# One memset more behind a block's scatters: GpSimd clears a spare tile after both of them in blocks 0 to 11

## The reference, cut to what matters

```
x = x + layernorm(attention(layernorm(x)))          # out = (q . sum k v) / (q . sum k)
x = x + layernorm(ffn(layernorm(x)))
ffn(x):
    shared = gelu(x @ Wfc_s + bfc_s) @ Wproj_s + bproj_s
    probs  = softmax(x @ Wr);  top 2, weights divided by their sum
    routed = sum over the two chosen experts e of
             weight_e * (gelu(x @ Wfc[e] + bfc[e]) @ Wproj[e] + bproj[e])
    return shared + routed
```

## Time and profile before

| | |
|---|---|
| median of three runs | 384.76 us |
| the profiled execution | 383.89 us, span 382.0 us |
| mean granted TensorE clock | 0.958 |
| PE busy | 336.9 us (88%) |
| DVE busy | 289.2 us (76%) |
| ACT busy | 256.6 us (67%) |
| POOL busy | 284.4 us (74%), 381 instructions |
| memsets of `spare` | 47, 20.6 us in all |

### The profile page before, as it was taken

The page is one execution under the profiler, slowest core; times in us unless marked ns, Lnnn a source line. Parts: engine busy times, 40 slices in busy tenths (PEclk is TensorE's granted clock), DMA queues, the critical chain, the costliest instruction groups (busy, mean ns, idle before and its releaser), DMA issues.

```text
span 382.0 us, 8164 instructions
## 1 busy us (share of the span) xinstructions
PE 336.9 (88%) x2497; PEld 292.0 (76%) x2497; DVE 289.2 (76%) x688; ACT 256.6 (67%) x692; POOL 284.4 (74%) x381
## 2 busy tenths in 40 slices
PE   7879797998999998989898995958999999989991
PEld 2538485796886868768598894948999999989971
DVE  4999999799999899999936663524554459787667
ACT  4949864887986978767246764216556666688764
POOL 8877898578788787888768888874666767866640
PEclk9969996999999999999999999886999999999997
DMA  6576767575473406143188387945788879988317
GB/s 194 166 218 168 174 180 123 115 207 133 145 194 104 140 29 199 36 135 101 33 257 259 113 226 204 243 149 159 217 263 257 251 242 367 350 246 263 125 52 205
DMA packets 53522, 69.18 MB, mean 181 GB/s; under 512 B 6365, under 2 KB 37386, under 8 KB 53482
## 3 DMA queue, kind: packets, MB, share of 16 engines
q1 hardware_dynamic: 47556, 58.58, 53.9%
q0 software_dynamic: 4544, 9.35, 7.2%
q10 hardware_dynamic: 1382, 0.79, 0.8%
HBM read 40.06 MB, written 18.15 MB: 152 GB/s over the span
## 4 chain that ended last, share of the span: by engine, by line
PE 39%; DVE 17%; ACT 11%; POOL 11%; issue 10%; another core or an unknown queue 6%; SPq 2%; DMA 2%; DVEq 0%; ACTq 0%; POOLq 0%
PE bS L1550 7%; PE bO L1550 7%; PE bO L1334 6%; DVE KV L1701 3%; ACT hs L1024 2%; DVE KV L1692 2%; POOL expert_lists L707 2%; DVE SH L2071 2%; PE bV L1523 2%; POOL Z L789 2%; PE bV L1525 2%; PE bV L1524 2%; DVE w_lo L2124 1%; POOL Z L794 1%
## 5 line engine op out<-in xcount | busy, mean ns | idle before, releaser
L830 POOL DMA_INDIRECT expert_results<-yb,yrow x78 | 77.5, 994 | 39.5 <-issue 19.2
L707 POOL DMA_INDIRECT expert_lists<-rows,pos x64 | 64.3, 1004 | 19.7 <-issue 17.7
L1701 DVE TENSOR_TENSOR_SCAN KV<-bS,KV 128x1024 f32<-128x1024 bf16 x32 | 72.8, 2277 | 0.6 <-POOL KV L733 0.3
L1334 PEld LDWEIGHTS bO<-wout_rot,Z 128*128 128x128 f32 x512 | 60.5, 192 | 8.1 <-POOL Z L789 4.5
L1334 PE MATMUL bO<-wout_rot,Z 128*128 128x128 f32 x512 | 63.0, 277 | 1.9 <-POOL Z L789 1.1
L2148 DVE COPY yrow<-xb 128x2 int32<-128x2 int32 x24 | 6.8, 284 | 47.0 <-PE bS L1550 17.0
L1153 ACT ACTIVATE hs<-bV,KV 128x256 f32<-128x256 f32 x56 | 21.9, 474 | 21.1 <-remote 10.0
L1550 PE MATMUL bO<-KV,hs 128*128 128x128 f32 x232 | 29.2, 276 | 2.9 <-ACT hs L1153 1.9
L1550 PEld LDWEIGHTS bO<-KV,hs 128*128 128x128 f32 x232 | 27.5, 192 | 3.6 <-ACT hs L1153 3.4
L1304 PE MATMUL bA<-w2s_sb,hs 128*128 128x128 f32 x224 | 28.8, 277 | 0.0
L1523 PE MATMUL bV<-x_lo,w_hi 128*128 128x256 f32 x80 | 24.4, 305 | 4.2 <-DVE x_lo L2127 3.5
(11 more groups left out here) (370 smaller groups left out, 997.4 us busy)
## 6 DMA issues: line engine op xcount, KB each, us to landing
KV<-packed_weights SPq DMA_DIRECT2D x21, 578.0 KB
Z<-packed_weights SPq DMA_DIRECT2D x18, 578.0 KB
xb<-expert_lists SPq DMA_DIRECT2D x39, 129.0 KB
vr<-vr SPq DMA_DIRECT2D x16, 224.0 KB, 2.5
shared<-expert_results SPq DMA_DIRECT2D x7, 512.0 KB
vr<-vr SPq DMA_DIRECT2D x16, 192.0 KB
vr<-vr SPq DMA_DIRECT2D x16, 160.0 KB
vr<-vr SPq DMA_DIRECT2D x16, 128.0 KB
```

The costliest lines, as they stand in the source:

```text
L707: g.indirect_dma_start(out=lists, out_offset=bass.IndirectOffsetOnAxis(ap=pos[:, m:m + 1], axis=0), in_=rows[:, m // TILES, m % TILES, :], ...
L830: g.indirect_dma_start(out=results, out_offset=bass.IndirectOffsetOnAxis(ap=yrow[n][:, c], axis=0), in_=yb[n][:, c, :], in_offset=None).th ...
L1334: ins = t.matmul(bO[:, j * D:(j + 1) * D], Z[:, d, j * P:(j + 1) * P], wout_rot[:, d], start=False, stop=True, skip_group_check=True)
L1701: v.tensor_tensor_scan(w, ps_keep, w, 0.0, ALU.mult, ALU.add).then_inc(s["kv_sum"], 1)
```

## The change

`SINGLE` is 2 x 6 = 12. In the blocks 0 to 11 `still()` follows both scatters of a block; in the blocks 12 to 26 it stands between the two as before, and from block 27 on there is none.

```
             AT_END = 4
             PAIRED = 27
+            SINGLE = 2 * NBUF
...
                         in_=yb[n][:, c, :], in_offset=None).then_inc(blk_scat[n], 16)
-                    if b < PAIRED and c == 0:
+                    if b < SINGLE or b < PAIRED and c == 0:
                         still()
```

## The result

The changed kernel takes **0.9943** of the time before (95% interval 0.9922 to 0.9963): 380.94 us against 382.91, medians of 20 runs each. By this ratio it is 2.2 us faster (1.4 to 3.0), about half the 4.0 us forecast; it leaves out executions that count as slow, one of the changed kernel's (384.26 us) among them, and the medians, which do not, are 1.97 us apart. That 380.8 was met almost to the digit is partly luck: the median of the three runs shown before lay 1.9 us above that of the 20.

What follows compares the result with a forecast made beforehand. Late TensorE signals, from GpSimd scatters directly following each other, were taken to cost blocks 3 to 11 up to 16.7 us. Net of later late blocks, 4.0 us off 383.89 gave 379.9, plus 0.87 a median of 380.8 us; range 370 to 387.

Steps and rivals of the forecast that it cites:

- the buffers bind: Block 8 needs block 2's buffer, whose second scatter ends at 243.7 plus 2.5 us landing, so it comes at 246.2.
- the debt: GpSimd's scatter work lagging VectorE at block 12, forecast at 12.5 us, to be worked off in the blocks behind.
- The way back: From block 12, single memsets again: late blocks of 7.4 us each until GpSimd has caught up at block 17.9, 289.1 us.
- The sum of 3.1 to 5.9 us: Net time earlier once GpSimd has caught up at block 17.9; everything after block 27 shifts along.
- the return: Time regained in blocks 3 to 11 by prompt signals at 3.42 us per block; block 11 14.5 us earlier.
- The choice of 4.0: Net saving in us taken for the whole kernel, nearer the lower end of 3.1 to 5.9.
- The price of up to 5.3 us: Twelve added memsets of 0.44 us each holding up VectorE's copies through the shared port, without VectorE's idle time.
- The whole return stays: Rival: signals stay prompt after block 12 too; block 11 14.5 us earlier, 370 us; chance 0.20.
- The memset does nothing: Rival: lateness comes from something coinciding, DMA traffic or GpSimd being behind; today's time plus up to 1 us, 384.8; chance 0.22.
- the gaps shrink: Rival: memsets leave 0.16 us free instead of 0.30; blocks 3 to 8 5.0 us slower, 390 us; chance 0.16.

Runs made afterwards that it cites:

- 27: Changed kernel with the memset behind both scatters in blocks 0 to 26, not only 0 to 11; ratio 1.0025 to the kernel before, 385.0 us.
- 18: Changed kernel with the memset behind both scatters in blocks 0 to 17, not only 0 to 11; ratio 0.9882 to the kernel before.
- read-back later: Changed kernel with memsets behind both scatters in blocks 0 to 26 and the read-back of results 1 to 2 blocks later; ratio 0.9899 to the kernel before.

## Why the prediction was right, and where it was off

**The cause.** The prediction put the late signals down to scatters too close together. The runs without memsets and with short ones bear that out. From block 2's addition to block 8's the kernel before takes 36.1 us. With gaps of 0.30 to 0.48 us between all block scatters it is 36.5 to 38.6, whatever stands in them; with 0.58 to 0.72 it is 24.9 to 29.7. The ratios agree: 1.0056 to 1.0131 with the short gaps, 0.9882 to 1.0033 with the long ones (without the run that adds memsets in the earlier iterations), though the intervals of the nearest two overlap. One profile alone does not size the effect: four kernels whose GpSimd program is the same up to block 11 (changed, 27, 18, read-back later) had 8.4, 3.6, 17.6 and 30.6 us of unnamed waits from 222 to 262 us. Traffic alone is not the cause: the DMA share is 0.96 in the first slow stretch now, with fewer late signals than at 0.81. The Trainium skill (DMA: Bandwidth & Descriptors, section "Issuing engines are not separate DMA queues") has all queues share the same engines; that may hold here, but by these two rows it is not what delayed the signals.

**Blocks 3 to 8.** Forecast: 3.42 us each until the buffers bind, block 8 at 246.2. Measured: 4.3 each, block 8 at 248.86 with a "remote" wait in front. I took the memset's gap as enough, from the stretch 201 to 222 us; it is at the edge, and 8.4 us of waits stayed.

**Block 12 and the debt.** Forecast block 12 at 259.9 with GpSimd 12.5 us behind. Measured 262.11, and GpSimd's first scatter of it at 274.87, 12.8 behind. The distance was right; both came later than forecast, by 2.2 and 2.5 us.

**The way back.** Forecast: late blocks of 7.4 us at once, GpSimd level at block 17.9. Measured: 7.3 us per late block, the nearest hit of all, but the signals stayed prompt until the first bare pair at 278.00 and some 6 us beyond (283.81 is the first late copy), so VectorE ran further ahead and GpSimd was level only at block 20. The sum of 3.1 to 5.9 us became 2.9 at block 26, 2.6 in the span and 2.2 in the ratio, all below its lower end. The mechanism was right and the return was put too large: 12.3 us earlier at block 12 and not 14.5. The choice of 4.0 was too high.

**VectorE's copies.** I costed them at nothing, because VectorE idles ahead of them. They are indeed held up:

```profile
227.26 0.69 DVE L2149 COPY yrow<-xb 128x2 int32<-128x2 int32 x1 [1.59 <-issue]
```

This copy, 0.17 us elsewhere, ends at 227.95, and a scatter beside it at 227.98 (227.01 + 0.97). The Trainium skill (SBUF — State Buffer, section "SBUF: two separate sides") has the loser of the shared ports wait for the whole instruction; the trace agrees. The price of up to 5.3 us that the prediction worked out from it did not show: blocks 15 and 16, with copies of 0.42 and 0.38 us, still took 3.42 us each.

**The rivals.** "The whole return stays" fails at 278 us. "The memset does nothing" and "the gaps shrink" fail with block 8. I gave 0.46 to faster by over 1%; 0.57% lies in the class of no change, which had 0.38.

## What to carry to other kernels

When an engine that is behind stops delaying others, it is still behind: ask by when it must be level, and what the work until then will cost. Here the six programs with memsets of 0.43 us or more behind both scatters of at least twelve blocks (without the one that adds them in the earlier iterations and comes to this stage 9 us later) let SP read back first between 303.85 and 306.61 us, whether signals were prompt or late on the way; the kernel before did at 307.87, the others at 309.55 to 312.42. And before a waiting time is put down to the order of instructions, change the length of what stands between.

## What the runs showed of the hardware

TensorE's signals reached ScalarE and VectorE late, by up to 12.8 us (the run without the passage's memsets), in and just behind stretches in which GpSimd issued indirect DMAs every 1.27 to 1.43 us. They left no wait of unknown origin where it did so every 1.71 us (258 to 283 us in the run with 27 blocks). Near 1.57 us both occur: in the changed kernel the copies of blocks 5 and 8 wait "remote", and those of blocks 4 and 7 are released by TensorE by name. Nor is it the signals alone: in the run without the passage's memsets TensorE's matmuls of block 5's second layer, between 237 and 249 us, come with eight pauses, 7.0 us in all, for which the profile shows no wait. Why all this is so stays open: no row shows where a signal waits.
